# A four-layer conditional residual stack on one core: when the second sample and the output weights are loaded around attention's begin

## The chip, the cores and the metric

The kernel runs on one core of one Trainium2 chip. The metric is device time in microseconds (us) of one execution, as the median of several runs. The engines named below are PE (matmul), DVE, ACT and POOL (elementwise work; POOL also issues the indexed gathers) and SP, which computes nothing here and issues the DMAs.

## The reference, cut to what matters

```python
x = x + cond_matmul(x, W0[itok])                   # 64 samples, 32 rows of 512 each
x = x + linear(x, W) + gated_lora(x, Wr, A, B)
x = x + cond_matmul(x, W2[itok])
# the last layer: attention of 32 query heads over a paged cache of 8 key heads
q, k, v = x @ Wq.T, x @ Wk.T, x @ Wv.T             # per head: rmsnorm and rope of q and k
kc = k_cache[block_table]                          # 16 pages of 32 rows for each of 64 samples
vc = v_cache[block_table]
scores = q @ concat(kc, k).T * SCALE               # masked beyond the sample's length
o = softmax(scores) @ concat(vc, v)
x = x + o @ Wo.T
```

All of it is computed in float32 accuracy: each float32 operand is split into two 16-bit parts (high and low), and a product takes three matmuls (high by high, high by low, low by high).

## The kernel before, in words

There are three stages, one after the other on the same core.

**Mixing** (0 to some 100 us of the trace) makes the first three layers and stages the split projection weights in the buffer `w`, 96 KB in each partition, as six chunks of 1024 output columns.

**Projections** runs over 16 tiles of 128 rows (four samples each). A tile has 12 blocks of 512 output columns: 8 of queries, 2 of keys, 2 of values. For block n PE does 12 matmuls (L1121 to L1123) into one of four PSUM banks and counts `blk_done`. ACT takes squares (L1163), DVE multiplies with the rotation tables (L1369, L1373), POOL adds (L1252), PE turns the result (L1102, three blocks later), ACT and DVE split it (L1142 and L1379) into one of four buffers `turned`, and SP stores that buffer to HBM (`q_parts`, `k_new_parts`; L971). Since there are four buffers, ACT may write the head of one block only after the store four heads back has landed (`out_q`). The rows are normalised by a per-row factor `inv`, which DVE makes at the end of a tile (L1346 to L1355, function `inverse`) and which ACT applies to the keys (`normalise_keys`, `proj_kr`). Beside this, six chunks per tile of the caches and of the output weights are split and stored (`craw` in, `cparts` out; L987, L993).

SP's queue is written out by hand, block by block: chunk store and load, head store, value stores at block 7. At the end of tile 12 SP loads all of sample 0 into `room` (`first_sample`). In the last tile, at block 7, it calls `second_sample`: the new keys, the query, four pieces of row scales, 16 pages of keys (each page's number is read by SP from a row in SBUF) and four pieces of fresh values, all at one go, into the first half of `w`, whose columns the blocks already done no longer need. POOL gathers the cached values by index: two parts of sample 0 early (`first_values`), the other two and the four of sample 1 in the last tile (`later_values`, by the table `LATER` from block number to parts).

**Attention** runs over 16 groups of four samples, eight units (key heads) for each sample, 512 units in all. A unit: PE makes scores (L1654, L1655), DVE adds the mask and takes the maximum (L1807), ACT takes the exponential (L1737), DVE normalises (L1824), PE turns the probabilities (L1663), ACT and DVE split them (L1733, L1831), POOL prepares the part of the new tokens (L1605, L1608), PE weighs the values (L1690 to L1693). PE works two to three units behind. From the second group on PE also projects the outputs of the group before (L1704) with the output weights. Samples alternate between `room` (even) and `w` (odd); SP loads sample b when the scores of sample b-2 have been used up (`load`), POOL gathers its values at the end of sample b-1. The output weights are 8 parts of 1 MB; the table `WO_BEHIND` says behind which sample's load SP issues which parts. Part c waits until part c-2 has landed.

## Time and profile before

| | us |
|---|---|
| median of 3 runs | 2151.07 (2150.94 to 2154.25) |
| the profiled execution | 2156.13 |
| its span in the trace | 2154.4 |
| last projection matmul begins / first score matmul begins | 741.45 / 768.04 |

The profiled execution is 5 us above the median, and 1.7 us of it lie outside the span. A sum of terms read from the trace stands against 2156.13; to come to a median it is taken off 2151.07.

The page is read from the top: which engine is busy for most of the span, then in which slices it is not, then the engines' timelines and the windows of those slices, for what ended the idle time.

### The profile page before, as it was taken

The numbers are of one execution on the slowest core, as the hardware profiler recorded it, in microseconds if no ns is written. First come the engines' busy times: TensorE is split into PE (matmuls) and PEld (weight loads), VectorE is DVE, ScalarE is ACT, GpSimd is POOL, SyncE is SP. The second block draws the span as 40 slices with busy tenths as digits, with TensorE's granted clock in tenths as the row PEclk, the third lists the DMA queues.
The fourth block names the chain that finished last, engine by engine and source line by source line (L and its number), as shares of the span: only waits on it lengthen the run. The fifth ranks groups of instructions, "written<-read, shape, count | busy, mean of one in ns | idle before, by whom it ended". The sixth has DMA issues, their size and how long they took to land.

```text
span 2154.4 us, 55692 instructions
## 1 busy us (share of the span) xinstructions
PE 2063.3 (96%) x17217; PEld 1349.2 (63%) x17217; DVE 1676.2 (78%) x4284; ACT 1477.9 (69%) x4204; POOL 1104.4 (51%) x1853
## 2 busy tenths in 40 slices
PE   5898999999999767999999999999999999999999
PEld 3444555555555445777777777777777777777775
DVE  7787888888887566777777777777777777777774
ACT  2575777777776566777777777777777777777774
POOL 4464656565665534454454545454454545454542
PEclk9999999999999979999999999999999999999999
DMA  9655787776677759888888888887888888888881
GB/s 347 194 198 167 235 236 243 234 234 199 217 230 248 257 179 307 256 258 250 250 248 256 245 247 257 250 248 245 259 248 250 251 250 248 252 254 249 246 243 57
DMA packets 417498, 513.97 MB, mean 239 GB/s; under 512 B 67252, under 2 KB 313908, under 8 KB 416181
## 3 DMA queue, kind: packets, MB, share of 16 engines
q1 hardware_dynamic: 379828, 375.65, 57.1%
q0 software_dynamic: 37376, 134.76, 19.1%
q8 instruction: 142, 2.33, 0.5%
q14 instruction: 152, 1.24, 0.2%
HBM read 413.77 MB, written 92.54 MB: 235 GB/s over the span
## 4 chain that ended last, share of the span: by engine, by line
PE 60%; DMA 1%; DVE 1%; SPq 1%; issue 1%; ACT 0%; POOL 0%; DVEq 0%; POOLq 0%; ACTq 0%
PE att_scores L1654 15%; PE att_y L1704 15%; PE att_tr L1663 11%; PE att_o L1690 5%; PE att_o L1691 5%; PE att_o L1692 5%; PE att_o L1693 1%; PE att_tr_new L1669 1%; PE att_scores L1655 1%; DMA w<-v_parts,att_idx 1%; DVE att_prob L1807 1%; SPq L126 0%; DMA room<-k_parts 0%; SPq L132 0%; DVE att_tpl L1831 0%
## 5 line engine op out<-in xcount | busy, mean ns | idle before, releaser
L1807 DVE CUSTOM_DVE_ANT_0 att_prob<-att_scores,att_mask 128x544 f32<-128x544 f32 x512 | 370.9, 724 | 293.0 <-PE att_scores L1655 246.9
L1733 ACT ACTIVATE att_tph<-att_tr 128x512 f16<-128x512 f32 x512 | 306.3, 598 | 328.6 <-PE att_tr L1663 319.8
L1737 ACT ACTIVATE att_prob<-att_prob,att_col,rscale 128x544 f32<-128x544 f32 x512 | 430.8, 841 | 55.6 <-DVE att_col L1813 19.4
L1605 POOL CAST att_parts<-att_norm 128x96 f16<-128x96 f32 x512 | 135.8, 265 | 575.0 <-issue 557.0
L1831 DVE TENSOR_TENSOR att_tpl<-att_tr,att_tph 128x512 f16<-128x512 f32 x512 | 350.2, 684 | 1.0 <-ACT att_tph L1733 0.9
L1663 PE MATMUL att_tr<-ident,att_norm 128*128 128x128 f32 x2048 | 326.4, 282 | 0.0
L1704 PE MATMUL att_y<-w,att_ot 128*128 128x512 f16 x1152 | 307.5, 379 | 0.0
L1252 POOL TENSOR_TENSOR proj_rn<-proj_ra,proj_rb 128x512 f32<-128x512 f32 x128 | 190.5, 1488 | 203.7 <-DVE proj_rb L1373 169.0
L1690 PE MATMUL att_o<-att_tph,w 128*128 128x128 f16 x1536 | 284.4, 219 | 4.0 <-DMA w<-v_parts,att_idx 1.9
L1692 PE MATMUL att_o<-att_tph,w 128*128 128x128 f16 x1536 | 284.4, 219 | 0.0
L1691 PE MATMUL att_o<-att_tpl,w 128*128 128x128 f16 x1536 | 284.4, 219 | 0.0
L1824 DVE TENSOR_SCALAR att_norm<-att_prob,att_col 128x544 f32<-128x544 f32 x512 | 254.2, 496 | 1.0 <-issue 1.0
L1663 PEld LDWEIGHTS att_tr<-ident,att_norm 128*128 128x128 f32 x2048 | 215.8, 141 | 61.8 <-issue 1.3
L1163 ACT ACTIVATE proj_square<-proj_blk 128x128 bf16<-128x128 f32 x640 | 169.2, 285 | 121.7 <-PE proj_blk L1123 121.7
L1654 PE MATMUL att_scores<-room 128*128 128x512 f16 x768 | 224.8, 383 | 16.5 <-PEq L814 7.4
L1654 PE MATMUL att_scores<-w 128*128 128x512 f16 x768 | 220.5, 377 | 0.8 <-DVE att_col L1807 0.4
L1595 POOL DMA_INDIRECT w<-v_parts,att_idx x186 | 183.7, 988 | 47.6 <-POOL att_idx L1593 23.6
L1690 PEld LDWEIGHTS att_o<-att_tph,w 128*128 128x128 f16 x1536 | 150.6, 98 | 31.4 <-issue 2.2
L1369 DVE TENSOR_TENSOR proj_ra<-proj_blk,proj_ta 128x512 f32<-128x512 f32 x160 | 110.1, 688 | 76.2 <-ACT proj_square L1163 71.1
L1613 POOL TENSOR_TENSOR att_ot<-att_of,att_ot 128x512 bf16<-128x512 f32 x128 | 157.0, 1226 | 3.5 <-ACT att_of L1733 3.5
L1121 PE MATMUL proj_blk<-w,xt 128*128 128x512 f16 x384 | 146.3, 381 | 6.8 <-PEq L249 6.8
L1691 PEld LDWEIGHTS att_o<-att_tpl,w 128*128 128x128 f16 x1536 | 150.6, 98 | 0.0
(226 smaller groups left out, 5266.2 us busy)
## 6 DMA issues: line engine op xcount, KB each, us to landing
room<-k_parts SPq DMA_DIRECT2D x512, 128.0 KB
w<-k_parts SPq DMA_DIRECT2D x512, 128.0 KB
q_parts<-proj_turned SPq DMA_DIRECT2D x128, 256.0 KB, 3.5
v_new_parts<-proj_vp SPq DMA_DIRECT2D x64, 256.0 KB
room<-q_parts SPq DMA_DIRECT2D x32, 512.0 KB
w<-q_parts SPq DMA_DIRECT2D x32, 512.0 KB
w<-in_w_t SPq DMA_DIRECT2D x12, 1024.0 KB, 16.8
room<-in_k_t SPq DMA_DIRECT2D x8, 1024.0 KB, 6.2
```

The costliest lines, as they stand in the source:

```text
L1252: g.tensor_tensor(out[:, :], ra[n % 2][:, :], rb[n % 2][:, :], ALU.add).then_inc(sum_done, 1)
L1654: mm(old, a, k, start=start, stop=stop)
L1663: last = nc.tensor.transpose(tr[q][:, c * P:(c + 1) * P], old[:, c * P:(c + 1) * P], ident[:, :])
L1690: mm(out, vh, th, start=(c == 0), stop=False)
L1691: mm(out, vh, tl, start=False, stop=False)
L1692: mm(out, vl, th, start=False, stop=False)
L1704: last = mm(y_ps[:, :], ot[p][:, a, h, :], wo_of(h, h + 1)[:, 0, w, :], start=(h == 0 and start), stop=(h == HQ - 1 and stop))
L1733: copy = lambda out, in_, **kw: nc.scalar.activation(out, in_, ACT.Copy, **kw)
L1737: nc.scalar.activation(prob[q][:, :], prob[q][:, :], ACT.Exp, bias=col[q][:, 1:2], scale=row_scale(i), accum_out=col[q][:, 2:3]).then_inc( ...
L1807: v.tensor_tensor_reduce(out=prob[q][:, :], in0=sc[q], in1=mask[bi % 2][:, at:at + LK], scale=1.0, scalar=-3.0e38, op0=ALU.add, op1=ALU.ma ...
L1824: v.tensor_scalar(out=norm[q][:, :], in0=prob[q][:, :], scalar1=col[q][:, 3:4], scalar2=TOP, op0=ALU.mult, op1=ALU.mult).then_inc(norm_don ...
L1831: v.tensor_tensor(tpl[q][:, :], tr[q][:, :], tph[q][:, 0:L], ALU.subtract).then_inc(tl_done, 1)
```

## The change

The sample-1 load is cut into pieces. `first_sample` (end of tile 12) now also loads sample 1's row scales. In the last tile, `second_sample(n)` is called behind each block n from 2 on: two pages at each of blocks 2 to 9, the query at block 5, the new keys at block 6, the fresh values at block 10; each waits for the blocks whose columns it writes over. SP reads page numbers at blocks 2 and 6. POOL's gathers go one to a block, at blocks 4 to 9, those of sample 1 first; before, they went 1, 2, 2, 1 at blocks 6 to 9. Two of the value buffers move to another place in `w`. The output weights: parts 0 to 4 are issued at attention's begin (before: 0 to 2), parts 5, 6, 7 behind samples 2, 3, 4 (before: 3 and 4 behind sample 2, then 5, 6, 7 behind samples 3, 4, 5), and each waits until the part before it has landed.

```diff
         keys1 = take([NPP + 1, HK, 2, PS], F16)
         query1 = take([HK, 2, P], F16)
-        values1 = [take([HK, 2, HD], F16) for _ in range(LC)]
         fresh1 = take([HK, HD], BF16)
+        values1 = [take([HK, 2, HD], F16) for _ in range(EV)]
+
+        skip = 2 * KD * 2 * WC
+        take = taker(columns[:, skip:half], half - skip)
+        values1 += [take([HK, 2, HD], F16) for _ in range(LC - EV)]
...
-        LATER = {6: (2,), 7: (3, 4), 8: (5, 6), 9: (7,)}
+        LATER = {4: (4,), 5: (5,), 6: (6,), 7: (7,), 8: (2,), 9: (3,)}
...
                 load_fresh(sp, 0, fresh[0], vn_d, early)
-
-            def second_sample():
-
-                sp.wait_ge(early, SAMPLE)
-                sp.wait_ge(blk_done, (NT - 1) * BLK + BLK // 2)
-                load_sample(nc, sp, 1, 0, 1, keys[1], query[1], rscale[1], page0, k_d, kn_d, q_d, rs_d, early)
-                load_fresh(sp, 1, fresh[1], vn_d, early)
+                load_row_scales(sp, 1, rscale[1], rs_d, early)
+
+            second_pages = []
+
+            def second_sample(n):
+
+
+                if n == 2:
+                    sp.wait_ge(early, SAMPLE + 16 * HB)
+                sp.wait_ge(blk_done, (NT - 1) * BLK + n // 2 * 2)
+                half, at = divmod((n - 2) * 2, NPP // 2)
+                if at == 0 and half < 2:
+                    second_pages[:] = pages_of(nc, 1, half, page0)
+                if half < 2:
+                    for j in (at, at + 1):
+                        load_page(sp, half * (NPP // 2) + j, second_pages[j], keys[1], k_d, early)
+                if n == 5:
+                    load_query(sp, 0, 1, query[1], q_d, early)
+                if n == 6:
+                    load_new_keys(sp, 1, keys[1], kn_d, early)
+                if n == BLK - 2:
+                    load_fresh(sp, 1, fresh[1], vn_d, early)
...
-                    if t == NT - 1 and n == BLK // 2 + 1:
-                        second_sample()
+                    if t == NT - 1 and n >= 2:
+                        second_sample(n)
...
-                if c == EV:
+                if c == LC:
                     pool.wait_ge(early_values, 16 * EV)
-                    pool.wait_ge(blk_done, (NT - 1) * BLK + BLK // 2)
+                    pool.wait_ge(blk_done, (NT - 1) * BLK + 4)
+                if c == LC + EV:
+                    pool.wait_ge(blk_done, (NT - 1) * BLK + 6)
...
-        WO_BEHIND = {0: (0, 1, 2), 2: (3, 4), 3: (5,), 4: (6,), 5: (7,)}
+        WO_BEHIND = {0: (0, 1, 2, 3, 4), 2: (5,), 3: (6,), 4: (7,)}
...
             def load_wo(c):
-
-                after(sp, wo_in[c % 2], 16 * (c // 2))
+                if c:
+                    sp.wait_ge(wo_in[(c - 1) % 2], 16 * ((c - 1) // 2 + 1))
```

SP's queue in the last tile, before, from block 7's stores into the burst. `w` is the room of sample 1, `q_parts` the stored query heads when it stands on the left and the loaded query when on the right, `v_new_parts` the fresh values:

```order
L971 DMA q_parts<-proj_turned 128x1024 [waits proj_heads_low,proj_heads_high] x2
L979 DMA v_new_parts<-proj_vp 128x1024 [waits proj_v_low,proj_v_mid]
L979 DMA v_new_parts<-proj_vp 128x1024 x3
L121 DMA w<-k_new_parts 128x512 [waits proj_block,early_samples]
L123 DMA w<-q_parts 128x8x256
L126 DMA rscale<-q_row_scales 32x8 x4
L128 TENSOR_LOAD room
```

Behind that stand the 16 pages and the four pieces of fresh values, and only then the next head store. The same place after, blocks 6 to 8:

```order
L999 DMA q_parts<-proj_turned 128x1024 [waits proj_heads_low,proj_heads_high]
L139 TENSOR_LOAD room [waits proj_block]
L146 ISA
L146 DMA w<-k_parts 128x512
L146 ISA
L146 DMA w<-k_parts 128x512
L127 DMA w<-k_new_parts 128x512
L999 DMA q_parts<-proj_turned 128x1024 [waits proj_heads_low,proj_heads_high]
L1007 DMA v_new_parts<-proj_vp 128x1024 [waits proj_v_low,proj_v_mid]
L1007 DMA v_new_parts<-proj_vp 128x1024 x3
L146 ISA [waits proj_block]
```

Between two head stores there are now at most two pages with one smaller load, or the four value stores.

SP's queue at attention's begin, before:

```order
L1577 DMA att_page_row<-in_pages 1x1024
L1559 DMA w<-wo_parts 128x4096 [waits att_pages_in]
L1559 DMA w<-wo_parts 128x4096
L1559 DMA w<-wo_parts 128x4096 [waits att_wo_in0]
L121 DMA room<-k_new_parts 128x512 [waits att_exp,att_scores]
```

and after:

```order
L1622 DMA att_page_row<-in_pages 1x1024
L1604 DMA w<-wo_parts 128x4096 [waits att_pages_in]
L1604 DMA w<-wo_parts 128x4096 [waits att_wo_in0]
L1604 DMA w<-wo_parts 128x4096 [waits att_wo_in1]
L1604 DMA w<-wo_parts 128x4096 [waits att_wo_in0]
L1604 DMA w<-wo_parts 128x4096 [waits att_wo_in1]
L127 DMA room<-k_new_parts 128x512 [waits att_exp,att_scores]
```

Two more parts stand ahead of sample 2's load, and four of the five wait for their predecessor's landing.

## Rows read from the trace of the kernel before

**Rows 1.** The page, part 1: busy us (share of the span) xinstructions.

```profile
PE 2063.3 (96%) x17217; PEld 1349.2 (63%) x17217; DVE 1676.2 (78%) x4284; ACT 1477.9 (69%) x4204; POOL 1104.4 (51%) x1853
```

**Rows 2.** Windows: stretch and length, busy us per engine (instructions), PEclk, DMA share, GB/s.

```profile
725.00:730.00 5.00, 5.00 (x29) 2.78 (x28) 4.32 (x7) 2.82 (x13) 3.54 (x3) 1.00 0.48 141
735.00:740.00 5.00, 5.00 (x29) 2.83 (x28) 3.86 (x8) 2.53 (x13) 4.21 (x5) 1.00 1.02 354
741.80:768.04 26.24, 2.26 (x9) 1.46 (x9) 4.68 (x7) 6.11 (x16) 5.33 (x5) 0.54 0.78 272
```

**Rows 3.** PE's timeline between stages: start, us, what, [idle before it <-releaser].

```profile
741.45 0.38 PE L1123 MATMUL proj_blk<-w,proj_xt 128*128 128x512 f16 x1
758.31 2.28 PE L1102 MATMUL proj_tq<-ident,proj_kr 128*128 128x128 f32 x8 [16.48 <-ACT proj_kr L1142]
768.04 0.59 PE L1654 MATMUL att_scores<-room 128*128 128x512 f16 x1 [7.45 <-PEq L814]
```

**Rows 4.** ACT's timeline at the last block of the last tile.

```profile
755.35 0.60 ACT L1142 ACTIVATE proj_turned<-proj_tq 128x512 f16<-128x512 f32 x1 [14.20 <-DMA q_parts<-proj_turned]
...
756.98 2.44 ACT L1142 ACTIVATE proj_kr<-proj_kr,proj_inv 128x128 f32<-128x128 f32 x8
```

**Rows 5.** SP's timeline (DMAs issued) over the last tile's end and attention's begin.

```profile
729.15 2.61 SPq L979 DMA_DIRECT2D v_new_parts<-proj_vp  x4
731.86 0.61 SPq L121 DMA_DIRECT2D w<-k_new_parts  x1
...
737.88 8.85 SPq L132 DMA_DIRECT2D w<-k_parts  x16
...
749.23 0.86 SPq L971 DMA_DIRECT2D q_parts<-proj_turned  x2
...
762.69 2.26 SPq L979 DMA_DIRECT2D v_new_parts<-proj_vp  x4
...
769.53 5.17 SPq L1559 DMA_DIRECT2D w<-wo_parts  x3
```

**Rows 6.** DVE's timeline: the last step of the factor that normalises the keys.

```profile
743.62 0.15 DVE L1355 TENSOR_TENSOR proj_inv<-proj_ss 128x8 f32<-128x8 f32 x1
```

**Rows 7.** Around sample 0's load: SP's and ACT's timelines; PE's waits, 634 to 704 us.

```profile
646.97 1.81 SPq L139 DMA_DIRECT2D room<-v_new_parts  x4
...
652.93 0.72 ACT L1142 ACTIVATE proj_chunk_parts<-proj_chunk,up 128x512 f16<-128x512 f32 x1 [3.84 <-DMA proj_chunk<-in_wo_t]
...
PE proj_tq L1102 <- DVE proj_turned L1379: 2.0, 2, 1.7
```

**Rows 8.** PE's timeline: idle times in attention's first group that end on a DMA.

```profile
819.64 0.29 PE L1690 MATMUL att_o<-att_tph,room 128*128 128x128 f16 x1 [4.42 <-DMA w<-v_parts,att_idx]
...
831.66 0.39 PE L1654 MATMUL att_scores<-w 128*128 128x512 f16 x1 [0.37 <-DMA w<-k_parts]
...
855.86 0.61 PE L1654 MATMUL att_scores<-room 128*128 128x512 f16 x1 [4.14 <-DMA room<-k_parts]
```

**Rows 9.** SP's timeline in attention's first group: the loads of samples 2, 3 and 4.

```profile
788.49 0.32 SPq L121 DMA_DIRECT2D room<-k_new_parts  x1
...
792.24 10.19 SPq L132 DMA_DIRECT2D room<-k_parts  x16
...
804.33 0.90 SPq L1559 DMA_DIRECT2D w<-wo_parts  x2
...
809.55 7.67 SPq L126 DMA_DIRECT2D rscale<-q_row_scales  x4
...
832.48 6.97 SPq L126 DMA_DIRECT2D rscale<-q_row_scales  x4
```

**Rows 10.** Landing times of parts 0 (issued 769.53) and 4 (804.8); sample 2's first scores.

```profile
DMA to landing us min/median/max: 4.8/4.8/4.8
...
DMA to landing us min/median/max: 12.9/12.9/12.9
...
L1654 PE MATMUL att_scores<-room x8: 376/376/379, 807.2 to 811.9; 128*128 128x512 f16 x8
```

29 lines of the change are left out of this document (19 added, 10 removed).

## The prediction, made before the changed kernel ran

> **What bounds the kernel now.** I read the page first: PE is busy for 96% of the span [rows 1], so a change off PE's path is worth nothing, and a gap on PE is worth its whole length, since the work behind it is PE-bound and does not give it back. Then I looked for PE's gaps. The largest lies where projections end and attention begins: in 26.2 us PE does 2.3 us of work [rows 2]. PE's timeline shows its parts [rows 3]: the last projection matmul ends at 741.83 (741.45 + 0.38); PE waits 16.48 us for ACT's `proj_kr`; after turning the keys it waits 7.45 us for the stage's end, which is the last stores and their landing. The smaller gaps lie in attention's first group, 4.42 us for gathered values, 0.37 and 4.14 us for pages of keys [rows 8]. Later groups show no such gap, because there PE has the output projection as well and takes longer over a sample.
>
> Why is `proj_kr` late? ACT stood for 14.20 us before a plain split of a turned head, until a store of `q_parts` had landed [rows 4]. That store was issued at 749.23 [rows 5]. Its data was there long before: SP was busy from 731.86 to 748.7 with sample 1's burst, 16.8 us in which nothing else on its queue moves [rows 5]. So **the bound of this stretch is the order on SP's queue**. DMA traffic stands right behind it: 354 GB/s with all 16 engines busy at 735 to 740, and only 141 GB/s ten us before [rows 2].
>
> **The change part by part.**
>
> *The burst leaves the path.* With the head store early, ACT would do its split when block 11 ends. Two results are then needed before the keys can be normalised: block 11 through ACT (741.83 plus two copies that took 756.98 - 755.84 = 1.14 us, so 742.97), and the factor from DVE, ready at 743.62 + 0.15 = 743.77 [rows 6]. The later one counts. `proj_kr` begins at 743.77 instead of 756.98 [rows 4]: **-13.2 us**. What follows it (turn, split, store of keys, rest of the values, stores at 762.69, landing, barrier) is one chain of dependences that keeps its length, 768.04 - 756.98 = 11.1 us, so attention would begin at 754.8.
>
> *The pieces between the stores.* SP now does, ahead of the head store that ACT waited for: at block 6 a read of page numbers (about 1.1 us, the gap between rows before the pages), two pages at 8.85/16 = 0.55 us each and the new keys at 0.6, together 2.8 us; at block 7 two more pages, 1.1 us. The value stores ended at 731.76 [rows 5]; add 3.9, and 0.4 for the chunk store: the head store is issued at about 736.1. Stores issued into the saturated queue at 749 landed in about 6.1 us (749.23 to the release at 755.35 [rows 4, 5]). That gives 742.2. It is needed 1.63 us (756.98 - 755.35) ahead of 743.77, at 742.1. So it just fits, with nothing to spare, and the gathers and pages now come earlier and thicken the traffic of just these blocks. Bounds: 0 if it lands in time; +6.9 us if it takes the 12.9 us of the slowest landing that I found [rows 10] (736.1 + 12.9 - 742.1). I take **+1.0**, near the row of 6.1, which was measured at the same saturation.
>
> *Row scales move to sample 0's burst.* Four more issues at about 0.47 us (the neighbouring four took 1.81 [rows 7]) lengthen it by 1.9 us. It is not free there: the chunk load behind it came so late that ACT idled 3.84 us and PE lost 2.0 us [rows 7]. A stall that already exists grows one for one. Bounds 0 and +1.9; I take **+1.9**.
>
> *POOL's gathers one to a block.* A gather costs POOL about 1 us of a block's 3, beside an add of 1.3 to 1.7; at block 5 a low part of 1.2 us comes to it, a little over a block, but PE needs the add only three blocks later. No cost on POOL. The new places in `w` cost nothing: same instructions, same sizes.
>
> *Output weights at attention's begin.* Part 0 is issued 1.5 us after the begin (769.53 against 768.04) and took 4.8 us with part 1 alongside [rows 10]. Alone it is no slower. Four links of 4.0 to 4.8 us put part 4's issue 17.5 to 20.7 us behind the begin; sample 2's load was released 20.45 us behind it (788.49 [rows 9]). So the new waits delay it by 0 to 0.3 us, and the part still under way may hold SP a few us at the row scales. The slack: its last page was issued at 802.43 (792.24 + 10.19), at about two more us it lands, 804.4, and sample 2's scores began at 807.2 [rows 9, 10]. 2.8 us of slack hide that: **0**, bounds 0 and +3.
>
> The Trainium skill (DMA: Bandwidth & Descriptors, section Bandwidth) states 6.15 us for 1 MB moved alone and advises to batch; this speaks against one part at a time. Four links of 6.15 would put part 4's issue 26.1 us behind the begin, and after the slack some 2.8 us of stall; the trace's 4.8 us speaks for no stall, and the sum goes by it.
>
> *One MB less behind sample 2.* Before, parts 3 and 4 were issued at 804.33, just ahead of sample 3's load and beside sample 2's gathers [rows 9]. SP then took 7.67 us over four small loads, as if it had to wait for the 2 MB to drain, and PE waited 4.42 us for the last gather [rows 8]. At 354 GB/s [rows 2] 1.05 MB are 3.0 us. Sample 3's keys, which held PE for 0.37 us, come about as much earlier, so the gain can be kept. **-3.0**; bounds 0 (with one part ahead SP still stood 6.97 us [rows 9]) and -4.4. Parts 6 and 7 take the places of 5 and 6, so the 4.14 us before sample 4 stay.
>
> Sum: -13.2 + 1.0 + 1.9 + 0 - 3.0 = **-13.3 us**. Against the profiled execution: 2156.1 - 13.3 = 2142.8. Against the median: 2151.07 - 13.3 = 2137.8, so 2138.
>
> **The rivals.**
>
> *A: late stores.* The traffic of blocks 2 to 9 grows by what now moves earlier, six gathers of 0.5 MB among it, and the queue was full at 735 already [rows 2]. If the store lands in about 11 us rather than 6.1, 5 us come back: -8.3, 2142.8. For it: the 12.9 us landing [rows 10]. Against it: pages spread over blocks 2 to 9 start when the DMAs have room.
>
> *B: the chain of output weights comes late* and sample 2's keys hold PE by some 3 us: -10.3, 2140.8. For it: SP stands behind a part under way at 809.55 and 832.48 [rows 9]. Against it: both stood with gathers beside them.
>
> *C: bytes, not order, bound the last tile.* Between 741.8 and 768.04 the DMAs moved 26.24 us x 272 GB/s = 7.1 MB [rows 2]. Only the last stores must come behind block 11: four of heads and one of a chunk at 0.26 MB and four of values at 0.26, some 2.4 MB. The other 4.7 MB must now go through ahead of 741.8. If there is room for only a third of it, 3.1 MB are left, 8.8 us at 354 GB/s: -4.5, 2146.6, hardly to be told from no change. For it: the share of 1.02 at 735 to 740. Against it: the 141 GB/s at 725 to 730, which leave 213 GB/s free; in the 20 us from 715 that is 4.3 MB, nearly all that is to be moved.
>
> *D, slower: SP is held by the full queue between the pages.* At 809.55 SP took 7.67 us for four issues that take 1.9 when unhindered [rows 9]: 5.8 us for one such hold. In the changed last tile the same can happen behind the query (block 5), the value stores (7), the pages of 8 and the fresh values (10), each time ahead of a head store for which ACT waits. Four holds are 23 us: -13.3 + 23 = +9.7, 2160.8. The point from which it decides is the third hold. Against it: in the old burst SP issued pages at 0.55 us each although the DMAs were saturated [rows 2, 5].
>
> *E: the change does not do what it says*, for instance because ACT's wait is released by another store. It would leave 2151. The store order on SP leaves little room for that.
>
> **How the numbers follow.** Forecast 55% (2134 to 2141 by its own bounds), A 15%, B 8%, C 9%, D 8%, E 5%. The likeliest is 2138. The range runs from 2133 (-13.2 - 4.4, no cost for stores and row scales: 2133.5) to 2146, which takes in A and B and leaves out C, D and E but for their edges. A measurement of this kernel can tell about 0.2%, 4.3 us, from no change. Faster by more: forecast, A, B and part of C, 0.80. Within: most of C, E and a weak D, 0.13. Slower: D, 0.07.
>
> **What would show it.** PE's wait before turning the keys is 16.5 us now; it should be 2 to 4 us, released by ACT, with ACT's own wait for a store under 2 us; attention should begin about 10 us earlier (757 to 759). SP should show pages in pairs between stores, and no issue over 2 us. The DMA share should be near 1.0 already from 725, and lower after 750. At sample 0's load PE should lose near 4 us, not 2. Five parts should be issued about 4 to 5 us apart, sample 2's load not later than 21 us behind the begin, and the wait for gathered values near 1.5 us. I am wrong if ACT waits longer than 3 us for stores in the last tile, if SP's small issues stretch to 5 us and more there, or if samples 2 and 3 show new waits for keys.

## The result, and the profile after

| | before | changed |
|---|---|---|
| median | 2152.61 us (12 runs) | 2146.93 us (12 runs) |
| ratio, 95% interval | | 0.9977 [0.9969, 0.9986] |
| the profiled execution | 2156.13 | 2147.16 |
| its span | 2154.4 | 2145.4 |

The change makes the kernel 5 us faster (3.0 to 6.7 by the interval). I had predicted 13.3 us; 2146.93 lies just outside the range of 2133 to 2146. A second comparison, made later with five runs, gave 0.9962 [0.9949, 0.9975], 8 us, again short of the forecast.

PE's timeline of the changed kernel, to be held against [rows 3] and [rows 7] (start, us, what, [idle before it <-releaser]):

```profile
656.12 1.09 PE L1145 MATMUL proj_tq<-ident,proj_rn 128*128 128x128 f32 x4 [2.54 <-DVE proj_turned L1424]
...
743.56 0.38 PE L1166 MATMUL proj_blk<-w,proj_xt 128*128 128x512 f16 x1
...
761.31 0.58 PE L1699 MATMUL att_scores<-room 128*128 128x512 f16 x1 [7.46 <-PEq L842]
```

The last projection matmul begins 2.1 us later than before, and attention begins 17.75 us behind it, not 26.6. The wait for `proj_kr` fell from 16.48 to 7.64 us, where I expected 2 to 4:

```profile
751.57 2.28 PE L1145 MATMUL proj_tq<-ident,proj_kr 128*128 128x128 f32 x8 [7.64 <-ACT proj_kr L1185]
```

ACT's timeline over the last blocks shows what is left. In the place of one wait of 14.20 us [rows 4] stand four, 6.3 us in all, three for head stores and one for the value stores of the tile before:

```profile
738.64 0.60 ACT L1185 ACTIVATE proj_turned<-proj_tq 128x512 f16<-128x512 f32 x1 [2.00 <-DMA q_parts<-proj_turned]
...
741.59 0.60 ACT L1185 ACTIVATE proj_turned<-proj_tq 128x512 f16<-128x512 f32 x1 [1.31 <-DMA q_parts<-proj_turned]
...
746.59 0.69 ACT L1185 ACTIVATE proj_v<-proj_blk,xcol 128x512 f32<-128x512 f32 x1 [2.26 <-DMA v_new_parts<-proj_vp]
...
748.61 0.60 ACT L1185 ACTIVATE proj_turned<-proj_tq 128x512 f16<-128x512 f32 x1 [0.76 <-DMA q_parts<-proj_turned]
...
750.24 2.44 ACT L1185 ACTIVATE proj_kr<-proj_kr,proj_inv 128x128 f32<-128x128 f32 x8
```

SP no longer stands in front of the head stores for 16.8 us at a stretch. Its timeline (DMAs issued) shows the value stores, a pair of pages, a chunk store and a head store one behind the other, where the burst stood [rows 5]. So between two head stores stand the value stores and a pair of pages, and at block 5 a pair of pages and the query (512 KB, as much as four pages), which is more than the text on the change says:

```profile
734.70 2.14 SPq L1007 DMA_DIRECT2D v_new_parts<-proj_vp  x4
737.02 1.15 SPq L146 DMA_DIRECT2D w<-k_parts  x2
738.22 0.71 SPq L1021 DMA_DIRECT2D wo_parts<-proj_chunk_parts  x1
739.03 0.42 SPq L999 DMA_DIRECT2D q_parts<-proj_turned  x1
```

What takes long now is the landing. These are the times from issue to landing of those four value stores, then of six head stores issued from 725 to 745, then of the one head store issued at 739.03, for which ACT waited 0.76 us; last, for comparison, of the head stores from 715 to 728 in the kernel before, when the burst had not begun:

```profile
DMA to landing us min/median/max: 6.0/7.2/10.2
...
DMA to landing us min/median/max: 3.2/8.5/10.4
...
DMA to landing us min/median/max: 9.5/9.5/9.5
...
DMA to landing us min/median/max: 3.1/3.3/3.4
```

The windows give the traffic (stretch and length, busy us per engine, PEclk, DMA share, GB/s): 407 GB/s with all DMA engines busy, against 366 in the same ten us before:

```profile
725.00:735.00 10.00, 10.00 (x55) 5.54 (x54) 7.33 (x13) 6.15 (x31) 8.67 (x9) 1.00 0.92 297
735.00:745.00 10.00, 8.94 (x47) 4.48 (x45) 7.16 (x13) 4.74 (x21) 6.95 (x6) 1.00 1.05 407
```

In attention's first group PE waits for other things than before [rows 8]. Sample 2's keys are late by 4.49 us; the waits of 4.42 us for sample 2's values and of 4.14 for sample 4's keys are gone:

```profile
805.19 0.61 PE L1699 MATMUL att_scores<-room 128*128 128x512 f16 x1 [4.49 <-DMA room<-k_parts]
...
835.90 0.23 PE L1735 MATMUL att_o<-att_tph,w 128*128 128x128 f16 x1 [2.33 <-DMA w<-v_parts,att_idx]
...
857.51 0.23 PE L1735 MATMUL att_o<-att_tph,room 128*128 128x128 f16 x1 [0.90 <-DMA w<-v_parts,att_idx]
```

SP's timeline shows why: the five parts of output weights took 21.4 us to issue, so sample 2's load began 22.8 us behind attention's begin and not 20.45 [rows 9]. Three of the four links between them took 4.7 to 4.9 us, the third 6.68:

```profile
762.66 21.39 SPq L1604 DMA_DIRECT2D w<-wo_parts  x5
784.15 0.37 SPq L127 DMA_DIRECT2D room<-k_new_parts  x1
...
785.04 3.77 SPq L122 DMA_DIRECT2D rscale<-q_row_scales  x4
```

To compare traces I read four lengths off PE's timeline: where the projections begin; how long tile 13 takes (the one behind sample 0's load; other tiles take 35.4 us); the **last stretch**, from the begin of the last tile's matmuls to attention's first score matmul; and how far behind attention's begin samples 4 and 8 start. From sample 8 to the end every trace takes 1212.0 to 1213.5 us, so nearly all differences lie in these. The lengths are those of the profiled execution, the medians those of all executions; the two can differ by some 6 us (e1's profiled execution took 2144.4 us, e4's 2139.4, e7's 2148.7).

| run | median us | ratio to before | projections begin | tile 13 | last stretch | sample 4 | sample 8 |
|---|---|---|---|---|---|---|---|
| before | 2152.6 | | 170.3 | 37.8 | 61.8 | 87.8 | 173.9 |
| e0 before, again | 2154.0 | 1.0006 [0.9997, 1.0014] | 169.7 | 37.5 | 60.7 | 87.5 | 172.9 |
| e3 weights' order alone | 2151.7 | 0.9995 [0.9986, 1.0004] | 169.1 | 37.4 | 61.0 | 87.2 | 171.3 |
| **changed** | 2146.9 | 0.9977 [0.9969, 0.9986] | 170.7 | 39.8 | 53.0 | 86.0 | 171.1 |
| e14 changed, again | 2144.8 | 0.9962 [0.9949, 0.9975] | 171.4 | 39.8 | 53.6 | 83.7 | 168.4 |
| e1 weights as before | 2148.8 | 0.9987 [0.9978, 0.9995] | 170.4 | 39.9 | 54.1 | 82.9 | 168.3 |
| e2 weights two in flight | 2146.0 | 0.9965 [0.9952, 0.9978] | 172.4 | 39.8 | 53.0 | 85.5 | 171.4 |
| e4 row scales in last tile | 2145.7 | 0.9964 [0.9951, 0.9977] | 166.8 | 37.8 | 53.4 | 83.9 | 170.3 |
| e5 gathers late | 2148.9 | 0.9972 [0.9960, 0.9983] | 170.2 | 42.1 | 54.9 | 84.6 | 170.3 |
| e6 pages early | 2149.6 | 0.9982 [0.9969, 0.9995] | 170.6 | 40.0 | 55.7 | 83.8 | 171.7 |
| e7 e2, e4 and e6 | 2143.1 | 0.9951 [0.9939, 0.9964] | 173.1 | 37.7 | 54.9 | 84.7 | 171.1 |
| e8 no gathers | 2137.0, one run | | 168.3 | 39.8 | 48.5 | 84.9 | 169.0 |
| e9 small pages | 2141.5, one run | | 168.2 | 39.8 | 51.8 | 84.4 | 169.8 |
| e10b before, small pages | 2148.1, one run | | 169.8 | 37.5 | 57.6 | 86.1 | 171.8 |
| e11 e2 and e4 | 2141.0 | 0.9943 [0.9928, 0.9958] | 168.7 | 37.6 | 53.8 | 82.2 | 166.3 |
| e12 and 4 to 7 later | 2140.2 | 0.9933 [0.9920, 0.9946] | 169.2 | 39.6 | 55.1 | 76.3 | 168.3 |
| e13 and four gathers later | 2138.1 | 0.9923 [0.9907, 0.9938] | 171.1 | 39.5 | 51.1 | 76.7 | 166.7 |
| e15 and 4 to 7 spread | 2138.0 | 0.9923 [0.9911, 0.9935] | 171.4 | 37.7 | 50.1 | 79.7 | 163.8 |
| e16 changed, weights spread | 2139.3 | 0.9926 [0.9913, 0.9938] | 171.8 | 40.1 | 53.7 | 76.8 | 164.0 |

The last stretch repeats to about 1 us in kernels with the same edit, sample 8 to 2 or 3 us. The begin of the projections moves by 6 us (so the mixing stage ends near 170 us, not at some 100) without a relation to the edits that I can see; it stands for much of the scatter of whole times.

### The profile page after: what moved, and what is told of

The parts are those of the page before. It is cut to its first block, busy times and chain, and to the rows that moved or that the text cites. A ratio compares the mean times of both kernels' runs of the same rounds, so it can differ in the third digit from the quotient of the medians.

```text
span 2145.4 us, 55693 instructions
## 1 busy us (share of the span) xinstructions
PE 2063.9 (96%) x17217; PEld 1350.3 (63%) x17217; DVE 1674.1 (78%) x4284; ACT 1477.5 (69%) x4204; POOL 1101.8 (51%) x1853
## 3 DMA queue, kind: packets, MB, share of 16 engines
q8 instruction: 142, 2.33, 0.5%
## 4 chain that ended last, share of the span: by engine, by line
PE 57%; DVE 3%; DMA 2%; SPq 1%; issue 1%; ACT 0%; DVEq 0%; POOL 0%; POOLq 0%; ACTq 0%
PE att_scores L1699 15%; PE att_y L1749 14%; PE att_tr L1708 10%; PE att_o L1735 5%; PE att_o L1737 5%; PE att_o L1736 5%; PE att_tr_new L1714 1%; PE att_o L1738 1%; DVE att_prob L1852 1%; PE att_scores L1700 1%; DMA w<-wo_parts 1%; DMA w<-v_parts,att_idx 1%; SPq L146 1%; DVE att_mask L1835 1%; DMA room<-k_parts 1%
## 5 line engine op out<-in xcount | busy, mean ns | idle before, releaser
L1206 ACT ACTIVATE proj_square<-proj_blk 128x128 bf16<-128x128 f32 x640 | 169.2, 285 | 120.6 <-PE proj_blk L1166 120.6
L1735 PEld LDWEIGHTS att_o<-att_tph,w 128*128 128x128 f16 x1536 | 150.7, 98 | 32.0 <-DMA w<-v_parts,att_idx 2.7
L1737 PEld LDWEIGHTS att_o<-att_tph,w 128*128 128x128 f16 x1536 | 150.7, 98 | 0.0
```

The source lines that it names most:

```text
L1735: mm(out, vh, th, start=(c == 0), stop=False)
L1737: mm(out, vl, th, start=False, stop=False)
```

## Experiments

**Theory, after the traces.** What holds the last stretch was the order on SP's queue before, and is DMA traffic now. **Rival:** it is still order: the pages stand in SP's queue ahead of the stores, in smaller pieces. Beside it, two side costs are in question, the row scales at tile 12 and the chain of output weights.

### The kernel before once more (e0), and its burst with little data (e10b)

> The kernel before, once more, for a second trace and for the spread. The first trace of it has 26.6 us between the last projection matmul and attention's first (741.45 to 768.04), samples 2, 3 and 4 beginning 39.2, 63.6 and 87.8 us after attention's begin, and a time of 2156.1, 3.5 us above the median of its twelve timed runs (2152.6). Theory: the stage change is the same within 1 us, and what varies from run to run is the group of waits for DMAs in attention's first 90 us. Rival: the stage change itself varies by 3 to 4 us, so that the 9.0 us between the two first traces overstate what the change does there, and about 6 remain.

The last stretch came out 1.1 us shorter, sample 8 came 1.0 us sooner and the projections began 0.6 us sooner: three small differences and not one large, so neither expectation held as it was put. The first trace of before was a slow one in each part. Its 9.0 us over the changed kernel's first trace overstate the change.

For e10b the pages of the burst shrink, not their number:

```diff
-            sp.dma_start(keys[:, half * (NPP // 2) + j].rearrange("p h two s -> p (h two s)"),
-                         k_d[ds(page, 1)].rearrange("o p m -> (o p) m")).then_inc(loaded, 16)
+            sp.dma_start(keys[:, half * (NPP // 2) + j].rearrange("p h two s -> p (h two s)")[:, 0:cols],
+                         k_d[ds(page, 1)].rearrange("o p m -> (o p) m")[:, 0:cols]).then_inc(loaded, 16)
...
-                load_sample(nc, sp, 1, 0, 1, keys[1], query[1], rscale[1], page0, k_d, kn_d, q_d, rs_d, early)
+                load_sample(nc, sp, 1, 0, 1, keys[1], query[1], rscale[1], page0, k_d, kn_d, q_d, rs_d, early,
+                            PG // 8)
```

> The kernel before with sample 1's 16 pages in the burst cut to 16 KB each (seven eighths of its cached keys left out), number and place of the DMAs as before. If the order on SP bounds the stretch there, SP still issues for 15 to 17 us, ACT still waits 11 us or more for the head store behind the burst, and the stretch from the last tile's begin to attention's begin is 58.5 to 61 us (61.8 and 60.7 in the kernel before). If bytes bound it, it falls to 55 us or less.

SP's timeline and then ACT's wait, in this run:

```profile
730.54 0.58 SPq L121 DMA_DIRECT2D w<-k_new_parts  x1
...
735.90 8.98 SPq L132 DMA_DIRECT2D w<-k_parts  x16
744.92 1.81 SPq L139 DMA_DIRECT2D w<-v_new_parts  x4
...
747.31 0.86 SPq L971 DMA_DIRECT2D q_parts<-proj_turned  x2
...
749.81 0.60 ACT L1143 ACTIVATE proj_turned<-proj_tq 128x512 f16<-128x512 f32 x1 [9.98 <-DMA q_parts<-proj_turned]
```

SP issues for 16.2 us although the pages carry an eighth of the bytes; the store behind it lands 2.5 us after its issue (747.31 to 749.81) where it took 6.1. ACT waits 9.98 us, not 11 or more, and the stretch is 57.6 us: both are 1 us short of what I expected from order alone, and the stretch is 2.6 us above the rival's 55. So order made most of the wait, and the bytes of the pages 3 to 4 us of the stretch. The premise of the prediction holds in the main, in one trace. (The first run of this kernel is told of at the end.)

### The last tile without the gathers (e8), and with little in the pages (e9)

```diff
-                    if t == NT - 1 and n in LATER:
-                        for c in LATER[n]:
-                            later_values(c)
...
-                    pe.wait_ge(early_values, 16 * 2 * LC)
+                    pe.wait_ge(early_values, 16 * EV)
```

> The changed kernel without POOL's six gathers in the last tile (3.1 MB); samples 0 and 1 therefore weigh what lies in those buffers, that part of the computation is left out. The stretch from the last tile's begin to attention's begin is 61.8 and 60.7 us in two traces of the kernel before, 53.0 in the changed kernel, and 53.0 to 55.7 in every variant so far, however pages and gathers were placed. Theory 1 (bytes): with the DMAs full from 730 to 750 the stores cannot land sooner, whatever the order; without 3.1 MB (8 us at 400 GB/s) all of ACT's waits of 6.3 us go and the stretch falls to 48.6 to 49.5 us, the floor that the dependences alone give (35.2 + 13.4). Theory 2 (order on SP): nothing on SP's queue changes, so the waits stay and the stretch is 52 to 53 us.

PE's timeline at the stage's end:

```profile
744.49 0.66 PE L1145 MATMUL proj_tq<-ident,proj_kr 128*128 128x128 f32 x4 [3.18 <-ACT proj_kr L1185]
```

The wait is 3.18 us, and attention begins 13.3 us behind the last projection matmul. No wait of ACT for a DMA is left in the last blocks, and the value stores at the same place of SP's queue land in 3.3 to 4.2 us instead of 6.0 to 10.2:

```profile
DMA to landing us min/median/max: 3.3/4.0/4.2
```

The stretch of 48.5 us is the floor of the prediction (61.8 - 13.2 = 48.6) to a tenth. SP's queue was untouched: **bytes, not order, hold the changed kernel above its floor.** Whether it is the gathers' bytes or the number of their packets, the run doesn't tell apart; both left with them. So did about 1 us of POOL's time for each, but ACT's waits in the changed kernel ended on landings and not on POOL.

For e9 the changed kernel's pages are cut in the same way as e10b's:

> The changed kernel with sample 1's 16 pages loaded to an eighth of their width (16 KB instead of 128 KB each, 1.8 MB less in all); the same number of DMAs in the same place of SP's queue. Seven eighths of sample 1's cached keys are left out, so its scores are not the reference's. Theory 1 (bytes): the stretch from the last tile's begin to attention's begin falls from 53.0 to 49 to 50.5 us. Theory 2 (order on SP): the issues still stand ahead of the stores, and it stays at 52 to 53 us.

51.8 us, between the two expectations: 1.8 MB less gave 1.2 to 1.8 us, and ACT still waited 1.79 us for the value stores and 1.25 for a head store. Half of the pages are issued ahead of 730, where the worst traffic begins, and five of the six gathers behind it; that this is why a megabyte of pages counts for less is argued, not shown. The windows of 735 to 745, first of e8, then of e9:

```profile
735.00:745.00 10.00, 6.82 (x38) 3.59 (x36) 6.62 (x14) 7.00 (x23) 5.17 (x4) 1.00 0.88 308
...
735.00:745.00 10.00, 6.21 (x33) 3.14 (x31) 5.16 (x12) 4.10 (x14) 5.75 (x5) 1.00 1.04 375
```

### Moving the same bytes: gathers late (e5), pages early (e6)

```diff
-        LATER = {4: (4,), 5: (5,), 6: (6,), 7: (7,), 8: (2,), 9: (3,)}
+        LATER = {6: (2,), 7: (3, 4), 8: (5, 6), 9: (7,)}
```

> The changed kernel with POOL's gathers at blocks 6 to 9 (1, 2, 2, 1) as before, not one to a block from block 4. ACT in the changed kernel waits 2.0, 1.3 and 0.8 us for head stores and 2.3 us for the value stores of tile 14, which took 10 us to land. Theory 1 (traffic): the stores land late because pages, query and gathers share the DMAs with them from 725 on; with two gathers fewer ahead of block 7 the value stores land 2 to 3 us earlier, and the gap shrinks to 15 or 16 us. Theory 2 (order on SP): they are late by the issues ahead of them on SP's queue; the gathers are not on it, and the gap stays 17.4 to 17.8. A third outcome: six gathers in 11 us on top of pages make it worse, 19 us and more.

The wait for the value stores fell from 2.26 to 1.06 us, as the traffic theory has it, but the head store behind block 11 met the gathers: ACT waited 6.14 us for it and the stretch was 54.9 us. The gap between the last projection matmul and the first score matmul was 19.7 us, the third outcome and not one of the two theories; the traffic moved and the wait with it. (Tile 13 took 42.1 us in this trace, with a stall of 4.14 us at sample 0's load, which this edit doesn't touch.) The ratio 0.9972 cannot be told from the changed kernel's.

```diff
-                half, at = divmod((n - 2) * 2, NPP // 2)
+                half, at = divmod((n - 2) * 4, NPP // 2)
...
-                    for j in (at, at + 1):
+                    for j in range(at, at + 4):
```

> The changed kernel with four pages behind each of blocks 2 to 5 and none behind 6 to 9. The DMAs are busy for 32% at 715 to 720 and for all of the time from 730 on. Theory 1 (traffic) and theory 2 (order on SP) both expect ACT's four waits (6.3 us in all) to shrink below 2 us, and the gap from 17.7 to 14 us; time 3 to 4 us below the changed kernel's. Rival: what binds is bytes through the whole tile, and the waits only move to block 6 or 7 (stores 4 and 5 late there): the gap stays above 16.5 us or the last tile grows beyond 35.2 us.

Both theories were wrong here, and the rival right:

```profile
746.18 1.09 PE L1145 MATMUL proj_tq<-ident,proj_rn 128*128 128x128 f32 x4 [5.10 <-DVE proj_turned L1424]
...
744.71 0.60 ACT L1185 ACTIVATE proj_turned<-proj_tq 128x512 f16<-128x512 f32 x1 [6.82 <-DMA q_parts<-proj_turned]
```

ACT waited 6.82 us for one head store, PE lost 5.1 us inside the last tile, which took 43.1 us and not 35.2 to its last matmul. The gap behind it shrank to 12.6 us, but the stretch as a whole was 55.7 us, 2.7 longer. A shorter gap at the stage's end alone would have told the opposite.

### The row scales (e4)

```diff
-                load_row_scales(sp, 1, rscale[1], rs_d, early)
...
-                    sp.wait_ge(early, SAMPLE + 16 * HB)
+                    sp.wait_ge(early, SAMPLE)
...
+                if n == 4:
+                    load_row_scales(sp, 1, rscale[1], rs_d, early)
```

> The changed kernel with sample 1's row scales loaded behind block 4 of the last tile and not at the end of tile 12. Three traces with them at tile 12 show tile 13 of the projections 39.8 to 39.9 us long, three without 37.4 to 37.8. Theory: tile 13 falls back to 37.4 to 37.8, the gap between last projection matmul and first score matmul stays 17.4 to 17.8 us, and the time is 2 us below the changed kernel's. Rival: the four issues cost as much in the last tile, where SP's small loads and the stores are late already, and the gap grows by 1 to 2 us, so that nothing is gained.

Tile 13 took 37.8 us, the stretch 53.4, so the loads cost nothing that can be seen in the last tile at block 4. The medians differ by 1.2 us (2145.7 and 2146.9), within scatter.

The 2 us are not made up as I had them. The stall of PE at this place grew only from 1.97 us in two pieces before (1.72 in e0) to 2.54 in the changed kernel (2.65 in e14). The rest shows in the windows behind it, first of before, then of the changed kernel:

```profile
655.00:665.00 10.00, 9.58 (x51) 5.19 (x52) 9.06 (x15) 7.70 (x39) 6.28 (x4) 1.00 0.98 352
...
655.00:665.00 10.00, 8.88 (x40) 4.84 (x41) 8.56 (x13) 7.37 (x38) 5.92 (x4) 0.83 1.04 357
```

and in one microsecond of the changed kernel:

```profile
656.00:657.00 1.00, 0.88 (x4) 0.85 (x5) 0.07 (x1) 0.90 (x8) 0.00 (x0) 0.50 1.14 374
```

TensorE's granted clock stood at 0.50 there, the lower of its levels (1.2 GHz in place of 2.4), and came back to 1.00 after 3.4 us; 40 matmuls were done in the ten us and not 51. e12 and e13 have no row scales at this place, but stalls of 2.45 and 2.13 us, a granted clock of 0.88 and 0.83 in the ten us behind them, and tiles of 39.6 and 39.5 us. e4, e11 and e15 stalled PE for 1.8 to 1.9 us in two pieces, the longer 1.5 to 1.7, kept 1.00, and took 37.6 to 37.8. So the loads cost 0.6 to 0.9 us of stall and, through the clock, 1.2 to 1.6 us more. All nine traces with the loads at tile 12 have the long tile, and two of the ten without: taking them away makes the short tile likelier, not sure.

### The output weights (e3, e1, e2)

> The kernel before with the new order of the output weights alone (0 to 4 at attention's begin, one in flight, then 5, 6, 7 behind samples 2, 3, 4). Theory: the stage change stays 26.6 us; attention's first group is as in the changed kernel, with a wait of 4 to 5 us for sample 2's keys and none for sample 4's, sample 8 starting 171 us behind the begin instead of 173.9: 2 to 3 us below the kernel before. Rival: the gain in attention came from the earlier begin, and this change alone is worth nothing or costs 1 to 2 us.

With the old stage change, the new order alone is worth nothing that can be measured: 0.9995 [0.9986, 1.0004]. Its trace shows the exchange that the changed kernel shows, stronger: sample 2's keys are late by 6.90 us, sample 4's are not, and sample 8 begins 1.6 to 2.6 us sooner.

```profile
810.51 0.61 PE L1654 MATMUL att_scores<-room 128*128 128x512 f16 x1 [6.90 <-DMA room<-k_parts]
```

e1 is the changed kernel with the old order of the weights:

```diff
-        WO_BEHIND = {0: (0, 1, 2, 3, 4), 2: (5,), 3: (6,), 4: (7,)}
+        WO_BEHIND = {0: (0, 1, 2), 2: (3, 4), 3: (5,), 4: (6,), 5: (7,)}
...
-                if c:
-                    sp.wait_ge(wo_in[(c - 1) % 2], 16 * ((c - 1) // 2 + 1))
+
+                after(sp, wo_in[c % 2], 16 * (c // 2))
```

> The changed kernel with the output weights loaded as before (parts 0 to 2 at attention's begin, two in flight, 3 and 4 behind sample 2). Theory: the stage change keeps its gain (17.7 us between last projection matmul and first score matmul instead of 26.6); the wait of 4.5 us for sample 2's keys goes, and the waits of 4.4 us for sample 2's values and of 4.1 for sample 4's keys come back, so samples 4's start lies near 87.8 us behind the begin instead of 86.0 and the time is 1 to 3 us above the changed kernel's, near 2149. Rival: the new order of the output weights gives nothing or costs something, and this one is as fast as the changed kernel or 1 to 3 us faster (2144 to 2147).

The median, 2148.8, is 1.9 us above the changed kernel's, as expected, though the intervals of the two ratios overlap. The trace was not: the wait for sample 2's values came back (2.91 us), that for sample 4's keys hardly (0.27 us), and sample 4 began 82.9 us behind the begin, not 87.8. In this part of the kernel, traces of one kernel differ by as much as the edit. e2 keeps the new places and lets two parts be in flight (the lower half of e1's diff alone):

> The changed kernel, with parts 0 to 4 still at attention's begin, but two in flight as before instead of one. Theory: four links of 5.3 us made part 4's issue 21.4 us late; in pairs the five parts are issued within 12 to 15 us, sample 2's load starts when the scores release it (20.4 us behind the begin), its small loads take 2 us instead of 3.8, and the wait of 4.5 us for its keys shrinks below 1 us. Sample 4 starts 82 to 84 us behind the begin instead of 86.0, and the time is 2 to 4 us below the changed kernel's. Rival: the keys are late by the bytes and not by the chain; the wait moves to sample 2's values or to sample 3's keys and the time stays within 1 us.

SP's timeline shows the chain gone, 12.12 us for five issues in place of 21.39:

```profile
764.67 12.12 SPq L1604 DMA_DIRECT2D w<-wo_parts  x5
...
784.03 0.32 SPq L127 DMA_DIRECT2D room<-k_new_parts  x1
```

Sample 2's keys no longer held PE, samples 2 and 3 began at 39.3 and 59.3 us, but PE then waited 6.56 us for sample 4's keys, and sample 4 began at 85.5. That the chain delayed sample 2's load in the first trace is shown (22.8 us behind the begin there, 20.8 here); the gain was given back, as the rival said, though at sample 4's keys and not where it had put it. The median of 2146.0 is not told apart from 2146.9.

```profile
848.81 0.61 PE L1699 MATMUL att_scores<-room 128*128 128x512 f16 x1 [6.56 <-DMA room<-k_parts]
```

### The changed kernel again (e14)

> The changed kernel once more. The stretch from last tile to attention should be 52.5 to 53.5 us again, tile 13 39.8, and sample 2's keys late by 4 to 5 us. If the medians' difference (5.5 us) is right, attention's first eight samples take 172 to 174 us here instead of 171.1, or the begin of the projections, which varied between 166.8 and 173.1 us without relation to the kernel, lies later; if the traces' 9.0 us are right, the median here is near 2144.

Stretch 53.6, tile 13 39.8, but sample 2's keys held PE for only 0.52 us and sample 3's for 4.15:

```profile
802.48 0.39 PE L1699 MATMUL att_scores<-room 128*128 128x512 f16 x1 [0.52 <-DMA room<-k_parts]
...
825.48 0.61 PE L1699 MATMUL att_scores<-w 128*128 128x512 f16 x1 [4.15 <-DMA w<-k_parts]
```

The median was 2144.8, near the 2144 that the traces asked for. The stage change repeats, and which of samples 2 to 4 waits in attention does not.

The traces say more on the wait for sample 2's keys. Here the chain of five parts was faster than in the first trace of the changed kernel:

```profile
763.94 19.45 SPq L1604 DMA_DIRECT2D w<-wo_parts  x5
```

Four links took 19.1 us in e14, and 19.0 to 19.1 in e4 and e5, 4.7 to 4.8 each. In the changed kernel's first trace, e3, e8 and e9 the third link took 5.9 to 7.1 us, and part 4 was issued 21.7 to 22.7 us behind attention's begin; in these four traces PE waited 4.5 to 6.9 us for sample 2's keys. In e14, e4, e5 and e6 part 4 was issued at 20.4 to 21.1, and the wait was 0.5 to 2.1 us. So the wait goes with the chain, and one slow link makes it long; why the third link is slow in half of the traces stays open.

### Combinations (e7, e11, e12, e13, e15) and one table on the changed kernel (e16)

> Three edits on the changed kernel: pages four at a time behind blocks 2 to 5, row scales of sample 1 behind block 9 of the last tile, and the output weights two in flight (0 to 4 at attention's begin). If the three costs are separate they add: 2.2 us at tile 13, 3.5 us in the gap between stages, and 1 us from the weights (2146.9 and 2146.0 were the medians with one and with two in flight), so the time is near 2140 and certainly below 2143. Rival: the gain of an earlier begin is given back in attention's first group, where the loads of samples 2 to 4 bind; sample 8 then starts over 172 us behind the begin instead of 168 to 171, and the time stays near 2145.

2143.1, not 2140: the three did not add. The stretch was 54.9 us, 1.3 to 1.9 longer than in the changed kernel, with the early pages as in e6. Without them, and with the row scales behind block 9:

> The changed kernel with two edits that helped singly: sample 1's row scales behind block 9 of the last tile (not at tile 12), and the output weights two in flight. Pages stay two to a block, since four to a block made the stretch 2 to 3 us longer. Expected: tile 13 at 37.4 to 37.8 us, last stretch 53 to 53.5 us, no wait over 1 us for sample 2's keys; ratio to the kernel before 0.994 to 0.995, the fastest so far (two edits and early pages: 0.9951). Rival: row scales behind block 9 delay the last head stores by 2 us, the stretch is 55 us and the ratio 0.9955 or worse.

0.9943, median 2141.0, but the stretch was 53.8 us, and the sooner sample 8 (166.3) may be scatter. Next, on top of e11 (e12), the output weights leave the loads of samples 2 to 4 alone:

```diff
-        WO_BEHIND = {0: (0, 1, 2, 3, 4), 2: (5,), 3: (6,), 4: (7,)}
+        WO_BEHIND = {0: (0, 1, 2, 3), 5: (4, 5), 6: (6,), 7: (7,)}
```

> Row scales behind block 9 of the last tile, output weights two in flight, and now parts 0 to 3 at attention's begin, 4 and 5 behind sample 5, 6 and 7 behind samples 6 and 7, so that none moves beside the loads of samples 2 to 4. Theory: the waits for DMAs in attention's first group come from 1 MB parts in front of those loads; they go (5 us in the variant with parts 5 to 7 there), sample 8 starts 163 to 165 us behind the begin instead of 166.3, time 2 us below that variant's 2141.0. Rival: the loads of samples 2 to 4 are bound by themselves, and it stays at 2141 within 1 us; or a part comes late for the projection in group 1 and PE waits there.

Sample 4 began at 76.3 us, 6 us sooner, with no wait for a DMA before it; behind the two parts at sample 5 PE waited 4.57 us for sample 6's keys, and sample 8 began at 168.3. Time 2140.2. The rival was right on the time, the theory on the waits of samples 2 to 4. The trace also has a head store for which ACT waited 5.90 us in the last tile, a stretch of 55.1 us and the long tile 13, so its time doesn't show what the weights alone gave. In e13 POOL also gathers sample 1's four parts at attention's begin:

```diff
-        LATER = {4: (4,), 5: (5,), 6: (6,), 7: (7,), 8: (2,), 9: (3,)}
+        LATER = {6: (2,), 7: (3,)}
...
+            pool.wait_ge(early_values, 16 * LC)
+            for c in range(LC):
+                g.indirect_dma_start(out=values[1][c][:, :, :].rearrange("p h two d -> p (h two d)"),
+                                     out_offset=None, in_=v_d,
+                                     in_offset=bass.IndirectOffsetOnAxis(v_idx[:, LC + c:LC + c + 1].bitcast(U32), 0)
+                                     ).then_inc(early_values, 16)
...
-                    pe.wait_ge(early_values, 16 * 2 * LC)
+                    pe.wait_ge(early_values, 16 * LC)
+                if isinstance(n, int) and n == HK:
+                    pe.wait_ge(early_values, 16 * 2 * LC)
```

> As the run with the output weights later, and POOL gathers sample 1's four parts at attention's begin, where the DMAs have room, and only the two missing parts of sample 0 in the last tile (2.1 MB less there). Byte theory: ACT's waits for stores in the last tile shrink below 2 us in all and the stretch falls from 53 to 49 or 50 us, time 3 us below the run without this edit, near 2136. Rival: the bytes are only moved: four gathers and four parts of weights compete ahead of sample 1's values, PE waits for them at unit 8 or sample 2's keys are late, and the 3 us are given back.

The stretch fell to 51.1 us, not to 49 or 50, and ACT's waits for stores to 2.9 us in all, not below 2; PE did not wait for sample 1's values. Four of six gathers away gave about half of what all six gave. With one part behind each of samples 4 to 7 (e15):

> As the run with four gathers at attention's begin, with the output weights' parts 0 to 3 at the begin and one part each behind samples 4 to 7. With two parts behind sample 5, sample 4 began 76.7 us behind attention's begin and sample 8 at 166.7, 6 us lost between samples 5 and 6. Theory: two parts in a row hold SP and sample 6's keys, one does not; sample 8 then begins 161 to 164 us behind the begin and the time is 2133 to 2135. Rival: any part beside a load in group 1 costs its bytes, the loss is only spread, sample 8 stays at 166 to 167 and the time at 2138.

Stretch 50.1, sample 8 at 163.8, both the best among the kernels that leave nothing out. The profiled execution, to which these lengths belong, took 2135.1 us, as expected; but the median of six, 2138.0, is that of e13 and 3 us above it. So in the medians nothing tells one part at a time from two. Last, the same placement alone, on the changed kernel (e16):

```diff
-        WO_BEHIND = {0: (0, 1, 2, 3, 4), 2: (5,), 3: (6,), 4: (7,)}
+        WO_BEHIND = {0: (0, 1, 2, 3), 4: (4,), 5: (5,), 6: (6,), 7: (7,)}
```

> The changed kernel with one edit: output weights' parts 0 to 3 at attention's begin, one part each behind samples 4 to 7 (before the edit: 0 to 4, and 5, 6, 7 behind samples 2, 3, 4), still one in flight. Theory: with four parts the chain ends 5 us before sample 2's load is due, the wait for sample 2's keys goes, and none of samples 2 to 4 meets a part: sample 4 begins 76 to 78 us behind the begin instead of 84 to 86, sample 8 at 162 to 164 instead of 168 to 171, time near 2140. Rival: given back in group 1; sample 8 at 168 and time 2145 or more.

As expected: PE's only wait for a DMA up to sample 5 was this one, where the changed kernel's were 4.49, 2.33 and 0.90 us.

```profile
861.92 0.39 PE L1699 MATMUL att_scores<-w 128*128 128x512 f16 x1 [0.81 <-DMA w<-k_parts]
```

Sample 4 began at 76.8 us and sample 8 at 164.0, the time was 2139.3, ratio 0.9926 [0.9913, 0.9938] against 0.9962 and 0.9977. **One line of a table is worth 8 to 11 us here by the ratios, about as much as the whole change or more** (8 and 5 us by the same two). In the traces 4.4 to 7.1 us of it stand, the sooner begin of sample 8. e13, e15 and e16 all beat both kernels; they can't be told from one another, so what moving four gathers and the row scales adds to the new table is not shown.

## Why the prediction was wrong

Term by term, with the means of two traces of before and two of the changed kernel:

- *The burst leaves the path, -13.2.* Right in mechanism, and in size once the traffic is out of the way: e10b shows SP's order as the main cause before, and the stretch came to 48.5 us when the gathers were taken out (e8). In the second trace of before (e0) PE waited 15.37 us for `proj_kr` and not 16.48, so there the term would be 12.1.
- *The pieces between the stores, +1.0.* **This is the step that failed.** The stretch fell from 61.8 and 60.7 to 53.0 and 53.6 us: 8.0 us, where this step and the one above gave 12.2. Against the floor of 48.5 us it cost 4.5 and 5.1 us, inside my bound of 6.9 but far from what I took. I carried over the landing time of 6.1 us that a store had shown in the old traffic to blocks into which gathers and pages were being moved. The head store for which I had worked it out was issued 30.7 us behind the last tile's begin, where I had 29.9, and landed 9.5 us later, not 6.1: of 4.2 us, 3.4 are landing time. And I looked at one store only. The value stores of tile 14, for which ACT waits before it may write tile 15's values, do not stand in the prediction at all; the last of them took 10.2 us to land and made ACT wait 2.26. Rival A named the mechanism of late stores, and rival C the bytes. C's count came out: from the last tile's begin to the last projection matmul's end the DMAs moved 8.0 MB before and 9.6 MB in the changed kernel, 1.5 MB more, which is the third of 4.7 MB that C supposed. Its price of 8.8 us was too high; C had charged every byte that is left to the stretch, and ACT waits only for some of the landings. D did not happen: the longest issue of SP in the last tile took 1.6 us in both traces.
- *Row scales, +1.9.* Right in size by luck, wrong in its make-up: tile 13 grew by 2.1 us (37.65 to 39.8), and e4 took it away. But I had it all as issue time, and the longer stall was under a microsecond of it; the rest was matmuls at the lower granted clock behind the stall, which the sum did not have.
- *Output weights at the begin, 0.* Its bound of +3 was the better value: sample 2's keys held PE for 4.49 us in the first trace of the changed kernel and 0.52 in the second (e14). Each part was issued 0.02 us after its predecessor had landed, so a link is a landing. In the second trace the four links took 19.1 us, within my 4.0 to 4.8 each; in the first they took 21.1, because the third landed in 6.67 us. By the Trainium skill (DMA: Bandwidth & Descriptors, section Bandwidth) 1 MB alone takes 6.15 us. Three of the five landings here, 4.7 to 4.9 us, lie well below that, two, 6.0 and 6.7, near it; part 4 was issued 22.4 and 20.5 us behind the begin, not the 26.1 that this figure gives, so that its stall of some 2.8 us lies between the two measured ones by luck. One part at a time is a cost: two in flight issued the same five in 12.1 us.
- *One MB less behind sample 2, -3.0.* The wait that I pointed at went, as predicted. The 4.14 us before sample 4, which I had left standing, went as well, in both traces. Taken together with the term above, sample 8 came 2.8 us sooner in the first trace and 3.7 in the mean of two. But e3 shows that the new order alone can't be measured (0.9995), so how much of this belongs to it stays open. The waits of this group depend on each other: in e2, with no wait at sample 2's keys, it stood at sample 4's, in e14 at sample 3's.

The pieces of the means sum to -8.0 + 2.1 - 3.7 = -9.6, and a begin of the projections 1.0 us later makes it -8.6. The two comparisons gave -5 and -8. What lies between, up to 4 us, I can't assign; the begin of the projections, on which the edits have no bearing that I know, varied by 6 us between traces.

I also gave the forecast too narrow a range. Its lower end assumed that all costs were zero, and its upper end left out any combination of a late store with late keys; both came in the first trace.

## What to carry to other kernels

When a burst is spread under other work, the issue slots are found by the order, but the bytes have to be counted too: compare what the stretch carries after the move with what the DMAs can carry, and expect landing times to grow for every transfer in it, above all for stores whose buffers are waited for. List all waits on landings in the stretch that gets the new traffic, not only the one that the trace shows as late. Large transfers that are needed late, such as weights for a later stage, belong behind the loads that have slack; here that was worth about as much as the spreading or more. Whether one or two go at a time made no difference that the medians show.

## What the runs showed of the hardware

- Behind tile 12, stalls of PE of 1.3 to 1.7 us left the granted clock at 1.00 (eight traces), stalls of 2.1 to 3.1 us (the longest in e6) had 3.4 us at 0.50 beside or behind them (ten traces), and one of 4.14 us (e5) had 6.8 us. A few tenths of a microsecond more of waiting cost over a microsecond more of work: a turn of four took 1.09 us there, and 0.66 in e8 at 1.00.
- A 1 MB load issued alone landed in 4.7 to 6.7 us (median 4.9, the changed kernel), with a second in flight in 5.1 to 7.1 (median 6.7, e2). From the first issue to the last, five loads took 19.0 to 21.3 us one by one (eight traces) and 10.3 to 11.8 us in pairs (e2, e7, e11).
- SP's four loads of 1 KB took 2.1 to 2.7 us to issue at samples 2 to 5 of e12, and 6.9 us at samples 6 and 7 of the same trace, where parts of 1 MB had been issued up to 6 us before them. Over all traces they took from 1.8 to 7.7 us; that a part under way holds SP is likely by this, but some did not (2.0 to 2.7 us behind one in e3 and in the changed kernel).
- The first run of e10b's kernel took 7565.22 us. The first lines of its page, and a window of 20 us in the projections:

```profile
span 7563.5 us, 55692 instructions
...
PE 7529.4 (100%) x17217; PEld 3524.4 (47%) x17217; DVE 1730.4 (23%) x4284; ACT 1520.5 (20%) x4204; POOL 1083.8 (14%) x1853
...
2000.00:2020.00 20.00, 20.00 (x30) 6.56 (x29) 4.53 (x7) 5.10 (x21) 4.08 (x3) 1.00 0.21 66
```

PE did 30 matmuls in 20 us where it otherwise does 104 to 108, at a granted clock of 1.00; DVE and ACT were busy for 3% more than in the kernel before. A tile took 134.6 us and not 35.4. One of e6's twelve runs took 7566.33 us as well and is left out of its ratio. The cause was not found.
